# A fused attention and feed-forward layer on one core: the tasks of an attention block dealt anew over its four steps, moments and normalization in halves

## The reference

```python
x = x + tanh(g_xattn) * xattn(layernorm(x), ctx)   # windowed cross attention, 8 heads of 16 channels
x = x + tanh(g_ffn) * ffn(layernorm(x))            # 1024 -> 3584 -> 1024, weights are integers 0..15
```

## Time and profile before

| | us |
|---|---|
| median of 3 runs | 1631.78 (1631.67 to 1643.83) |
| profiled execution, its own time | 1639.15 |
| its span, from first to last instruction | 1636.9 |
| attention in it | from the start to about 435 |
| feed-forward part | from about 435 to the end |

### The profile page before, as it was taken

The page is one execution under the profiler, slowest core; times in us unless marked ns, Lnnn a source line. Parts: engine busy times, 40 slices in busy tenths (PEclk is TensorE's granted clock), DMA queues, the critical chain, the costliest instruction groups (busy, mean ns, idle before and its releaser), DMA issues.

```text
span 1636.9 us, 40533 instructions
## 1 busy us (share of the span) xinstructions
PE 1556.0 (95%) x16614; PEld 811.9 (50%) x16614; DVE 1450.1 (89%) x1425; ACT 1054.3 (64%) x1191; POOL 1256.5 (77%) x925
## 2 busy tenths in 40 slices
PE   5899999898789999999999999999999999999996
PEld 3566666666434444444444444444444444444444
DVE  4688877777598999999999999999999999999997
ACT  4577777777566666666666666666666666666652
POOL 4576776666546888888888888888888888888865
PEclk9899999999899999999999999999999999999999
DMA  4666665645434666666666666676666676667569
GB/s 121 161 149 147 172 150 139 156 125 140 128 117 114 148 152 153 152 153 152 152 152 155 154 154 155 153 154 147 153 152 153 146 155 156 151 154 155 116 180 321
DMA packets 192274, 249.50 MB, mean 152 GB/s; under 512 B 14446, under 2 KB 138030, under 8 KB 192074
## 3 DMA queue, kind: packets, MB, share of 16 engines
q1 hardware_dynamic: 168186, 163.74, 35.3%
q0 software_dynamic: 22752, 82.85, 28.8%
q10 hardware_dynamic: 1152, 0.33, 0.1%
HBM read 113.92 MB, written 16.78 MB: 80 GB/s over the span
## 4 chain that ended last, share of the span: by engine, by line
PE 90%; issue 4%; SPq 2%; POOL 1%; DVE 1%; DMA 1%; ACT 1%; ACTq 0%; DVEq 0%; POOLq 0%
PE bank L1182 69%; PE bank L1091 3%; PE bank L1080 3%; PE bank L1123 2%; PE bank L1043 2%; PE bank L1054 2%; PE bank L1039 2%; PE bank L1047 2%; PE bank L1101 1%; PE bank L1070 1%; PE bank L1051 1%; PE bank L1059 1%; POOL oacc L620 1%; SPq L396 1%; DMA gates<-in_g_ffn_dram 1%
## 5 line engine op out<-in xcount | busy, mean ns | idle before, releaser
L969 DVE SCALAR_TENSOR_TENSOR acc<-bank,scale,acc 128x1024 f32<-128x1024 f32 x784 | 969.6, 1279 | 52.0 <-PE bank L1182 15.1
L1182 PE MATMUL bank<-xT,w_int 128*128 128x512 f16 x3584 | 846.4, 379 | 7.5 <-DVE xT L920 3.7
L620 POOL TENSOR_TENSOR oacc<-oacc,d_part 128x1024 f32<-128x1024 f32 x219 | 536.7, 2455 | 54.0 <-ACT d_part L806 48.7
L1182 PEld LDWEIGHTS bank<-xT,w_int 128*128 128x128 f16 x3584 | 349.9, 98 | 431.6 <-DVE xT L920 5.3
L806 ACT ACTIVATE d_part<-bank,scale 128x1024 f32<-128x1024 f32 x219 | 244.1, 1115 | 200.9 <-PE bank L1182 197.0
L1182 PE MATMUL bank<-h_hi,d_int 128*128 128x512 f16 x896 | 339.6, 379 | 2.1 <-ACT d_part L806 1.8
L1182 PE MATMUL bank<-h_lo,d_int 128*128 128x512 f16 x896 | 339.6, 379 | 0.0
L806 ACT ACTIVATE d_more<-bank,scale 128x1024 f32<-128x1024 f32 x158 | 176.3, 1116 | 154.5 <-PE bank L1182 154.5
L564 POOL TENSOR_TENSOR raw_z<-raw_w,raw_z 128x512 int32<-128x512 int32 x168 | 225.6, 1343 | 19.1 <-DMA raw_z<-in_L_ffn_gate_z_dram 11.1
L622 POOL DMA_DIRECT2D oacc<-d_more x158 | 150.2, 951 | 114.1 <-ACT d_more L806 107.8
L610 POOL TENSOR_TENSOR h_lo<-acc,h_hi 128x1024 f16<-128x1024 f32 x56 | 129.5, 2312 | 23.1 <-ACT h_hi L788 23.1
(11 more groups left out here) (86 smaller groups left out, 1530.1 us busy)
## 6 DMA issues: line engine op xcount, KB each, us to landing
oacc<-d_more POOLq DMA_DIRECT2D x158, 512.0 KB, 5.2
raw_w<-in_L_ffn_gate_w_dram SPq DMA_DIRECT2D x56, 256.0 KB, 3.4
raw_z<-in_L_ffn_gate_z_dram SPq DMA_DIRECT2D x56, 256.0 KB, 4.2
raw_w<-in_L_ffn_up_w_dram SPq DMA_DIRECT2D x56, 256.0 KB, 3.4
raw_z<-in_L_ffn_up_z_dram SPq DMA_DIRECT2D x56, 256.0 KB, 4.0
raw_w<-in_L_ffn_down_w_dram SPq DMA_DIRECT2D x56, 256.0 KB, 2.9
raw_z<-in_L_ffn_down_z_dram SPq DMA_DIRECT2D x56, 256.0 KB, 3.7
vt<-vn_hl SPq DMA_DIRECT2D x64, 192.0 KB
```

The source lines that it names most:

```text
L620: nc.gpsimd.tensor_tensor(into, into, d_part[:, (n - 1) % 2, :], ALU.add).then_inc(d_added, 1)
L969: nc.vector.scalar_tensor_tensor(out=into, in0=pair[u % 4][:, :, :].rearrange("p h r -> p (h r)"), scalar=scale[:, par, i, m, k:k + 1], in ...
L1182: last = nc.tensor.matmul(dst[:, h, :], weights, rows_of(h, part), start=(part == 0), stop=(part == 1))
```

## The change

The tasks are dealt to the steps in another order, `v` now before `q`:

| step | before | after |
|---|---|---|
| 0 | x(second half), k, k | the same |
| 1 | q, q, t | v, v, t |
| 2 | v, v, t | q, q, t |
| 3 | x(first half), o, o | o, o, x(first half) |

The moments of x are taken one block later and in two halves: one at the end of step 0, the other after `soften` of step 1. Those of the finished row: one half at the end of step 1, the other after `soften` of step 2. Before, each stood whole at the end of a step (x in step 3, the row in step 0). On POOL `inverse_std` for x moves from behind step 3 to the head of step 1 of the next block, and the one for the row from step 1 to step 2; `set_residual` becomes two halves, behind `split_p` of steps 0 and 3. On ACT `norm_x` moves from the head of step 0 to the end of step 1, behind `take_pT`, as two instructions with a semaphore each, so that the first half of q waits for the first alone; `norm_row` moves from step 1 to step 2. `oT` has memory of its own. On SP `load_x` stands behind `place_v`.

```diff
-        oT = xn
+        oT = sb("oT", [P, T], fp32, att)
...
-            return ((x_end, k[:1], k[1:]), (q[:1], q[1:], t[:1]), (v[:1], v[1:], t[1:]), (x, o[:1], o[1:]))[s]
+            return ((x_end, k[:1], k[1:]), (v[:1], v[1:], t[:1]), (q[:1], q[1:], t[1:]), (o[:1], o[1:], x))[s]
...
                 if b + 2 < B:
-                    load_x(b + 2)
                     load_ctx(b + 2)
                 if b + 1 < B:
                     place_v(b + 1)
+                if b + 2 < B:
+                    load_x(b + 2)
...
-            def set_residual(b):
+            def set_residual(b, n):
...
-                nc.gpsimd.tensor_scalar(rows[b % 4][:, :], rows[b % 4][:, :], bo_g[:, 0:1], None, ALU.add)\
-                    .then_inc(residual_set, 1)
+                half = rows[b % 4][:, n * HALF:(n + 1) * HALF]
+                nc.gpsimd.tensor_scalar(half, half, bo_g[:, 0:1], None, ALU.add).then_inc(residual_set, 1)
...
-                    if s == 1 and b >= 2:
+                    if s == 1 and 0 < b < B - 1:
+                        inverse_std(b + 1, 0, mv_done, x_normed, shift_done)
+                    if s == 2 and b >= 2:
                         inverse_std(b - 2, 1, mv2_done, row_normed, shift2_done)
-                    if s == 2:
-                        set_residual(b)
                     split_p(b, s)
+                    if s in (0, 3):
+                        set_residual(b, s // 3)
                     if b == B - 1:
                         take_zero(0, s)
-                    if s == 3 and b + 2 < B:
-                        inverse_std(b + 2, 0, mv_done, x_normed, shift_done)
...
-                    act.wait_ge(projected, done("o", b - 3, 1) if b >= 3 else done("q", b - 1, 1))
-                nc.scalar.activation(xn[:, :], rows[b % 4][:, :], ACT.Identity, bias=shift[:, 0:1], scale=rstd[:, 0:1])\
-                    .then_inc(x_normed, 1)
+                    act.wait_ge(projected, done("q", b - 1, 1))
+                for n, normed in enumerate((half_normed, x_normed)):
+                    half = slice(n * HALF, (n + 1) * HALF)
+                    nc.scalar.activation(xn[:, half], rows[b % 4][:, half], ACT.Identity,
+                                         bias=shift[:, 0:1], scale=rstd[:, 0:1]).then_inc(normed, 1)
...
-                    if s == 0 and b + 1 < B:
-                        norm_x(b + 1)
...
-                    if s == 1 and b >= 2:
+                    if s == 1 and b + 1 < B:
+                        norm_x(b + 1)
+                    if s == 2 and b >= 2:
                         norm_row(b - 2)
...
                     soften(b, s)
+                    if s == 1 and 0 < b < B - 1:
+                        moments_x(b + 1, (1,))
+                    if s == 2 and b >= 2:
+                        moments_row(b - 2, (1,))
...
-                    if s == 0 and b >= 2:
-                        moments_row(b - 2)
-                    if s == 3 and b + 2 < B:
-                        moments_x(b + 2)
+                    if s == 0 and 0 < b < B - 1:
+                        moments_x(b + 1, (0,))
+                    if s == 1 and b >= 2:
+                        moments_row(b - 2, (0,))
...
-                    pe.wait_ge(x_normed, b + 1)
+                    pe.wait_ge((half_normed, x_normed)[n], b + 1)
```

More of the change, by code:

```diff
@@ L186, in flamingo_layer @@
         eps_added, root_taken = [sem("eps_added"), sem("eps2_added")], [sem("root_taken"), sem("root2_taken")]
[L187 to L188 removed]
+        stats_done, mv_done, shift_done, half_normed, x_normed = (
+            sem("stats_done"), sem("mv_done"), sem("shift_done"), sem("half_normed"), sem("x_normed"))
         stats2_done, mv2_done, shift2_done, row_normed = (
@@ L845, in _, with moments, moments_x @@
         def _(dve):
-            def moments(b, which, s_stats, s_mv):
-                for n in range(2):
+            def moments(b, which, s_stats, s_mv, halves):
+                for n in halves:
                     nc.vector.bn_stats(out=stats[:, which, n, :], in_=rows[b % 4][:, n * HALF:(n + 1) * HALF])\
                         .then_inc(s_stats, 1)
-                dve.wait_ge(s_stats, 2 * b + 2)
-                nc.vector.bn_aggr(out=mv[:, which, :], in_=stats[:, which, :, :]).then_inc(s_mv, 1)
-            def moments_x(b):
+                if halves[-1]:
+                    dve.wait_ge(s_stats, 2 * b + 2)
+                    nc.vector.bn_aggr(out=mv[:, which, :], in_=stats[:, which, :, :]).then_inc(s_mv, 1)
+            def moments_x(b, halves=(0, 1)):
                 dve.wait_ge(x_loaded[b % 2], 16 * (b // 2 + 1))
@@ L856, in moments_x, with moments_row @@
                     dve.wait_ge(shift_done, b)
-                moments(b, 0, stats_done, mv_done)
-            def moments_row(b):
+                moments(b, 0, stats_done, mv_done, halves)
+            def moments_row(b, halves=(0, 1)):
                 dve.wait_ge(emptied_proj, low_done("o", b, 1))
@@ L862, in moments_row @@
                     dve.wait_ge(shift2_done, b)
-                moments(b, 1, stats2_done, mv2_done)
+                moments(b, 1, stats2_done, mv2_done, halves)
             def soften(b, s):
@@ L897, in take_low @@
                     if n == 0:
-                        dve.wait_ge(residual_set, b + 1)
+                        dve.wait_ge(residual_set, 2 * b + 2)
                     row = rows[b % 4][:, n * HALF:(n + 1) * HALF]
```

## The result

The changed kernel takes 1648.25 us in the median of 5 runs (1642.31 to 1652.94), the kernel before 1632.61 in the runs beside it: ratio 1.0087, 95% interval 1.0050 to 1.0124. So it is slower, clear of noise, by less than the 1% that the prediction set as its limit for "same". A second set of runs of the same changed kernel gave 1645.03 us, 1.0068 (1.0044 to 1.0092). The profiled execution took 1652.94 us with a span of 1651.0, 14.1 more than the span before.

What follows compares the result with a forecast made beforehand. PE (95% busy) was taken to bound the kernel, losing 25.9 us to instruction-fetch gaps rather than DVE's lateness. Terms +18 - 1 - 1.5 - 4 + 0 = +11.5 us on 1631.8 gave 1643 us, range 1618 to 1660.

Steps and rivals of the forecast that it cites:

- The likeliest case: Whole kernel: the prediction's own sum of terms, +11.5 us to 1643 us, given chance 0.46.
- q waits for ACT: Start of q in step 2, blocks 1 to 14: PE waits 1.3 us each for norm_x's first half, +18 us.
- Transfers and fetches: Attention blocks: moving load_x behind place_v shifts where instruction fetches get in the way; 0 us, between a third less and more.
- Balance on DVE: Attention steps: spreading the moments evenly removes little lateness of DVE; -1 us, bounded by 0 and 4 us gained.
- Startup: Kernel start: the ctx load goes out ahead of x, shortening PE's 3.93 us wait; -1.5 us (0 to -3.9).
- Last block: Block 15: first weights leave earlier, POOL is free of its wait and the chain behind shortens; -4 us (0 to -5).
- The range of the sum: Whole kernel: bounds stated for the prediction's own sum of 1643 us, 1636 to 1652 us.
- q hardly waits: Start of q: ACT reaches norm_x in a gap's shadow or q is hidden otherwise, 18 us go; 1625 us, chance 0.10.
- The gaps are lateness: Attention: the issue gaps are lateness that the balance removes, and q's wait vanishes too; 1599 us, chance 0.10.
- Eased gaps: Attention: instruction-fetch gaps ease as x leaves the stretch of heavy transfers, half of 25.9 us gone; 1630 us, chance 0.14.
- The clock falls at the new wait: Step 2 and the first gap near it: lower granted clock, +12 us (1655) to +24 us (1667), chance 0.20.

Runs made afterwards that it cites:

- the whole normalization: The changed kernel with norm_x as one instruction of 1024 columns at the same place, instead of two halves: 1647.8 us, ratio 1.0086 to the kernel before.
- the kernel that repeats before: The kernel before with the first take_zero and its cast one step later in block 15, otherwise the same: 1629.40 us, ratio 0.9973.
- the table alone: The kernel before with only the new order of tasks (v in step 1, q in step 2) and oT in its own memory: 1651.27 us, ratio 1.0115.
- the two kernels with a misplaced load of x: The changed kernel with load_x back ahead of load_ctx and place_v, 1687.11 us; the kernel before with new task order, oT's own memory and load_x behind place_v, 1699.89 us.

## Why the prediction was right

The forecast was 1643 with +11.5 us; the median came out 1648.25 with +0.87%, and 1645.03 with +0.68% in the repeat: +14 and +11 us. The likeliest case is the one that came.

- **q waits for ACT** (+18, 14 x 1.3): the profile has 18.1 in 14 waits of at most 1.3. The walk through one step's head with ACT's place behind `pT` gave it, and 0.75 us for a half was right: two take 1.51. That PE gives nothing back is open: removing the wait gained 13 to 16 us of the 18, and moving `norm_x` ahead of `pT` only 3 to 6. Where all of v is placed and nothing else waits long, the three profiles in which q waits have gaps of 13.9 to 23.4 us (the change, its repeat, the whole normalization), those without that wait 21.3 or more. It may be that instructions arrive while PE stands, so that part of the wait is paid back in shorter gaps; single profiles don't show it.
- **Transfers and fetches** (0, bounds -9 and +9): before, 13 blocks lost (24.83 - 22.52) x 13 = 30 us over the undisturbed block. (That block runs from step 2 of block 5 to that of block 6; the caption there counts one too few, which changes no sum.) After, 340.28 / 13 = 26.18 us per block, against 22.52 + 1.3 = 23.82, is 2.36 x 13 = 31 us. In the repeat of the change it is 328.24 - 13 x 23.82 = 19 us, and in the kernel that repeats before 309.07 - 13 x 22.52 = 16. So the loss beside q stayed the same as far as two profiles each can tell, as the 0 says. That the gaps would move into step 2 was wrong: in the change they stay in steps 3 and 0. And 0 was the net of a bad order, a late load and late moments that fit together; I had taken each to be harmless by itself, and each isn't. In that the 0 was luck.
- **Balance on DVE** (-1, bounds 0 and -4): with the short second half before gained 5.5 us. That takes work away as well as lateness, so I take it as an upper end for what balance can bring, which is argued and not shown. The term was small but not shown to be as small as 1; and the 0.7 us that PE waits for the subtraction was no measure of what less work on DVE can bring.
- **Startup** (-1.5): came out at -0.1 in the one profile and -2.4 in the repeat. PE's wait of 3.93 us for ctx went, but in block 0 q now waits 5.79 us for `xn` (4.8 in the repeat), because ACT stands before `v_placed` on its way there:

```profile
36.22 0.60 ACT L656 ACTIVATE vn_hl<-bank 128x512 f16<-128x512 f32 x1 [5.38 <-DMA vt<-vn_hl]
```

  From there ACT runs without idle up to both halves of `xn`, so x itself has come in time. I had named ACT's wait and called it covered, and it isn't.
- **Last block** (-4): from the head of step 2 of block 14 to the end it is -3.2 with one 1.3 us wait at q inside, so -4.5; the repeat has -2.5, so -3.8. But from that head to the end the eight profiles with the change's last block have 1245.9 to 1250.6 us, before 1249.1: anything from -3.2 to +1.5. The moved `take_zero` alone gave before -4.4 us by its ratio (-8 to -0.5). That the wait went is shown, what it is worth is not resolved.
- **The range of the sum** was stated as 1636 to 1652. The bounds of its terms add up to 1626 to 1666; the result lies in either.

The rivals: *q hardly waits* is refuted by the 14 waits. *The gaps are lateness* is refuted by the 23.4 and 15.9 us that stay in the change; shortening the moments left 24.4 of 27.6. (15.9 is also below the 17 to 35 that the prediction wanted to see.) *Eased gaps* did not give its 1630, though one execution came near its gaps: 15.9 us where it has 13. The Trainium skill (Runtime: NRT & Kernel Launch, Instruction fetch mechanics) would have fetches mostly hidden. The traces here do not agree. The gaps stand inside groups that wait for no semaphore, up to 5.0 us long in the table alone, and each ends right behind a packet of the instruction queue. In the table alone PE stands from 226.29 to 231.29; the DMA view from 228.6 to 228.9 us has the start of the one packet of 16.4 KB that falls into it (packets, MB, share):

```profile
q8 instruction: 1, 0.02, 22.7%
```

The share is 1.09 us of one engine: the packet runs from 228.71 to 229.80, and PE goes on 1.49 us later. All 148 gaps of 0.8 us or more between 60 and 410 us in the fourteen profiles end 1.1 to 1.9 us after the end of such a packet (mean 1.45, standard deviation 0.14). At moments taken evenly over the kernel before, the last packet lies 2.0 us back with a deviation of 1.4. So the gaps are waits for instructions, as the prediction read them. The packets before gaps take no longer than others (1.10 and 1.09 us before) but start later behind the one before them (5.6 and 4.3 us). What holds them up isn't shown; that v's traffic has a part in it is what halving it suggests.

*The clock falls at the new wait* did not come in its form. Of the stretches of 5 us from 60 to 410 us of the kernel after, five are granted 0.78 or less: at 80, 240 (0.73), 315 (0.72), 365 and 395 us. Three of them (busy by engine, clock, DMA share, GB/s):

```profile
80.00:85.00 5.00, 4.93 (x142) 2.83 (x125) 2.94 (x5) 1.75 (x3) 1.74 (x3) 0.78 0.15 57
...
365.00:370.00 5.00, 4.86 (x85) 2.65 (x85) 3.83 (x6) 2.10 (x4) 2.33 (x4) 0.66 0.38 151
...
395.00:400.00 5.00, 4.39 (x58) 2.94 (x63) 2.70 (x4) 1.49 (x2) 2.84 (x2) 0.66 0.02 7
```

Before had three such (275, 300 and 330 us, at 0.66) and the repeat two. A stretch at 1.00 is at the level of 2.4 GHz; these are partly at 1.2. All lie behind gaps of a microsecond or more in steps 3 and 0, and the stretch with the 1.3 us at q, 14 times, isn't among them: the 16 transposes behind it, at 174.00, take the 1.06 us of full clock, not the 1.91 of the earlier trace rows. The rule of the Trainium skill (TensorE: Matmul & The Clock Gate, A second HAM failure mode) on frequent short idles would have wanted dips at q; this trace does not show them. In the two kernels with a misplaced load of x, where PE waits longer, the clock was granted less: 25.6 and 31.3 us by the sum above, 8.5 in the change.

## What to carry to other kernels

When a producer is moved behind another instruction of its engine, walk one step's head with both engines' rows: when the consumer is ready, when the producer's engine comes free, and how long its first half takes. That gave the wait to 0.1 us; and taking such waits away from the bounding engine gave back 13 to 16 us of 18. A load's place in a queue hangs on what frees its buffer and on who is first to need it, so move it together with both or not at all. And repeat a profile before reading gaps of a few microseconds: here the same program had 15.9 and 23.4 us of them.

## What the runs showed of the hardware

- Gaps inside groups of equal matmuls without a semaphore reached 5.0 us, and ended 1.1 to 1.9 us after a packet of instructions had landed. The timeline of the table alone:

```profile
231.29 0.30 PE L1123 MATMUL bank<-vt,pT 96*32 96x32 f16 x17 [5.00 <-issue]
```

- They vary between executions of one program while waits set by the order don't: 15.9 and 23.4 us beside 18.1 and 18.1.
- Two activations of 512 columns took 1.51 us together where one of 1024 took 1.24: 0.27 us for cutting one in two. PE did not wait for the second half: it has one wait at q per block.
- With a longer wait at q (24.1 us instead of 18.1) the ratio did not rise and the gaps were smaller (13.9 us). Whether PE's pause lets its instructions catch up, or it is chance between executions, stays open.
- Where PE waited for DVE 11 times, up to 9.3 us, the granted clock from 60 to 410 us was 31.3 us short of full by the sum above, before 5.1.
